# Another order of TensorE, VectorE and ScalarE between the down projection and the column a, and one z product moved ahead of the last output projection

## The reference

```
x = x + tanh(g_xattn[0]) * xattn0(layernorm(x), ctx)   # 32 heads of 128, 8 kv heads, rmsnorm on q and k, softmax
x = x + tanh(g_ffn[0])   * ffn0(layernorm(x))          # permute features, 16 blocks 32->128, gelu, 128->32, unpermute
x = x + tanh(g_xattn[1]) * xattn1(layernorm(x), ctx, ctx)
x = x + tanh(g_ffn[1])   * ffn1(layernorm(x))          # 8 experts 512x512, the best of 8 for each token

def xattn1(inp_q, inp_k, inp_v):                       # inp_k = inp_v = ctx, c = 128 channels (tokens), 8 groups of 16
    t, p, g = Wt @ inp_v, Wp @ inp_q, Wg @ inp_k       # for each batch, 128x128 times 128x512
    att = sum(p * g) over each group                   # one number for each batch and group
    y = blockdiag(Wz) @ (att * t)
    yn = (y - mean(y)) * rsqrt(var(y) + 1e-5)          # over each group
    return yn * gn_w + gn_b + inp_v
```

## Time and profile before

| | us |
|---|---|
| median of 3 runs | 797.38 (796.01, 797.38, 799.69) |
| profiled execution, its own time | 797.66 |
| its span (first to last instruction) | 795.9 |
| mean granted clock of TensorE | 0.982 |

### The profile page before, as it was taken

The page is one execution under the profiler, slowest core; times in us unless marked ns, Lnnn a source line. Parts: engine busy times, 40 slices in busy tenths (PEclk is TensorE's granted clock), DMA queues, the critical chain, the costliest instruction groups (busy, mean ns, idle before and its releaser), DMA issues.

```text
span 795.9 us, 12734 instructions
## 1 busy us (share of the span) xinstructions
PE 755.1 (95%) x3975; PEld 592.2 (74%) x3975; DVE 459.6 (58%) x1038; ACT 430.5 (54%) x1274; POOL 274.5 (34%) x431
## 2 busy tenths in 40 slices
PE   5999989899999999999999999999999987987997
PEld 3888877788888888888888888888887743555775
DVE  4786411556465656564655565656558764787652
ACT  4543315556556556555655655655555466557831
POOL 0331005234334233424423523433322438624242
PEclk9999999999999999999999999999999999797999
DMA  8545461132041140140131203203142135664232
GB/s 303 180 133 172 133 189 46 49 150 76 15 173 37 57 173 28 54 183 15 66 119 80 66 30 158 80 15 120 34 131 85 54 109 184 240 261 158 73 109 76
DMA packets 42126, 87.82 MB, mean 110 GB/s; under 512 B 5561, under 2 KB 26041, under 8 KB 38226
## 3 DMA queue, kind: packets, MB, share of 16 engines
q1 hardware_dynamic: 38884, 78.71, 28.7%
q0 software_dynamic: 3184, 8.41, 3.1%
HBM read 70.28 MB, written 35.57 MB: 133 GB/s over the span
## 4 chain that ended last, share of the span: by engine, by line
PE 71%; DVE 6%; ACT 3%; POOL 2%; DMA 2%; issue 1%; POOLq 0%; DVEq 0%; SPq 0%
PE banks L882 8%; PE banks L916 7%; PE banks L884 7%; PE banks L883 7%; PE banks L918 7%; PE banks L917 7%; PE banks L868 6%; PE banks L903 3%; PE banks L895 2%; PE banks L1831 2%; PE banks L1830 2%; PE banks L1832 2%; PE banks L927 2%; PE banks L929 2%; PE banks L928 2%
## 5 line engine op out<-in xcount | busy, mean ns | idle before, releaser
L592 ACT ACTIVATE p_sb<-p_sb,nmax 128x128 f32<-128x128 f32 x256 | 99.7, 391 | 62.7 <-DVE nmax L784 62.5
L587 ACT ACTIVATE oT_hi<-banks 128x512 fp32r<-128x512 f32 x64 | 38.2, 597 | 140.1 <-PE banks L929 140.1
L822 DVE SCALAR_TENSOR_TENSOR x_sb<-banks,tgates,x_sb 128x512 f32<-128x512 f32 x64 | 48.0, 749 | 70.8 <-PE banks L918 70.8
L690 POOL TENSOR_TENSOR v_lo<-v_raw,v_hi 128x128 fp32r<-128x128 f32 x64 | 29.5, 461 | 133.6 <-ACT v_hi L635 133.6
L779 DVE SCALAR_TENSOR_TENSOR p_sb<-banks,q_rstd,mask 128x128 f32<-128x128 f32 x256 | 71.5, 342 | 4.5 <-POOL q_rstd L83 4.0
L868 PEld LDWEIGHTS banks<-kT,qT_sb 128*128 128x128 f32 x512 | 67.7, 193 | 5.9 <-issue 0.5
L695 POOL TENSOR_TENSOR p_sb<-p_sb,rsum 128x512 f32<-128x512 f32 x64 | 66.5, 1040 | 15.2 <-DVE rsum L812 15.2
L868 PE MATMUL banks<-kT,qT_sb 128*128 128x128 f32 x512 | 68.2, 277 | 0.1
L768 DVE TENSOR_TENSOR oT_lo<-banks,oT_hi 128x512 fp32r<-128x512 f32 x64 | 44.1, 689 | 33.0 <-ACT oT_hi L587 33.0
L400 PE MATMUL banks<-w_hi,ctx_hi 128*128 128x512 f32 x128 | 54.1, 422 | 9.0 <-DVE ctx_lo L331 9.0
L816 DVE TENSOR_TENSOR pT_lo<-banks,pT_hi 128x512 fp32r<-128x512 f32 x64 | 44.2, 690 | 24.9 <-ACT pT_hi L610 24.9
(11 more groups left out here) (276 smaller groups left out, 1901.9 us busy)
## 6 DMA issues: line engine op xcount, KB each, us to landing
sorted_x<-in_empty SPq DMA_DIRECT2D x8, 2064.0 KB, 9.7
w_raw<-in_wq_l SPq DMA_DIRECT2D x8, 1024.0 KB, 5.1
w_raw<-in_wo_l SPq DMA_DIRECT2D x8, 1024.0 KB, 4.8
exp_w<-in_exp_w_l SPq DMA_DIRECT2D x8, 1024.0 KB, 9.3
kT_scr<-kT_st SPq DMA_DIRECT2D x16, 256.0 KB, 2.3
v_scr<-v_st SPq DMA_DIRECT2D x16, 256.0 KB, 2.3
xs<-sorted_x SPq DMA_DIRECT2D x15, 258.0 KB, 2.8
v_raw<-v_scr SPq DMA_DIRECT2D x14, 256.0 KB, 2.6
```

The costliest lines, as they stand in the source:

```text
L592: last = act.activation(p_sb[:, b % 2, h * P:(h + 1) * P], p_sb[:, b % 2, h * P:(h + 1) * P], ACT.Exp, bias=nmax[:, b % 2, h:h + 1], accum ...
```

## The change

The z product of batch 4 moves from the start of `middle` to a place ahead of the last output projection, into bank 6. On PE the gate weights and z means move ahead of y 0 to 3, and g 3 to 7 are put between the transposes of y. On DVE the gate column and the squares move ahead of the updates of x, and the first product moves behind all updates. On ACT the centring of z is put between the copies of g, and the third's seeds and the normalisations follow later in the list, two batches at a time. `normalise3` waits for the same things as before. Two waits of SP change places.

PE's order is now: g 0, 1; gate weights and z means; g 2; y 0 to 3; g 3; y 4, 5; g 4; y 6; g 5; y 7; p 0; g 6; p 1; g 7; p 2, 3; variance; p 4 to 7.

```diff
@@ attention
-        xT_ps, z_ps = [s.ps[i] for i in (0, 1, 4, 5)], [s.ps[i] for i in (0, 3, 0, 1)]
+        xT_ps, z_ps = [s.ps[i] for i in (0, 1, 4, 5)], [s.ps[i] for i in (0, 3, 0, 1, 6)]
...
+            def z4(u, b, g, odd):
+                if after(u, b, g, B - 1):
+                    pe.wait_ge(pT_lo_done, UNITS)
+                    z_product(4)
...
-                [(scores, 0), (sum_squares, 4), (z01, 0), (p_transpose, -1), (z2, -1), (o_proj, -2),
+                [(scores, 0), (sum_squares, 4), (z01, 0), (p_transpose, -1), (z2, -1), (z4, -2), (o_proj, -2),
                  (transpose_x, -4), (values, -1), (z3, -1)])
@@ middle, scalar
-            def normalise3(c):
-                act.wait_ge(xshift3_done, c + 1)
-                for b in range(*THIRDS[c]):
+            def normalise3(*bs):
+                for b in bs:
+                    act.wait_ge(xshift3_done, 1 if b < HB else b // 2)
                     reached(act, p_done, b - HB + 1)
...
-            for b in range(5):
-                copy_g(b)
+            copy_g(0)
+            copy_g(1)
+            copy_g(2)
+            centre(0, 1)
+            copy_g(3)
+            centre(2, 3, 4)
+            copy_g(4)
+            centre(5)
+            copy_g(5)
+            centre(6)
             seed3(0)
-            copy_g(5)
+            normalise3(0, 1)
+            seed3(1)
+            normalise3(2, 3)
             copy_g(6)
-            normalise3(0)
-            seed3(1)
-            centre(0, 1)
-            normalise3(1)
+            seed3(2)
+            normalise3(4, 5)
             copy_g(7)
-            seed3(2)
-            centre(2)
-            normalise3(2)
-            centre(3, 4, 5, 6, 7)
+            normalise3(6, 7)
+            centre(7)
@@ middle, vector
-            updates_with_stats(dve, s, update_x, x_done, bn_done, mv_done, xval3_done, THIRDS[:1])
-            negate_mean(0)
             dve.wait_ge(gmean_done, 1)
...
-            updates_with_stats(dve, s, update_x, x_done, bn_done, mv_done, xval3_done, THIRDS[1:2])
-            negate_mean(1)
-            product(0)
-            updates_with_stats(dve, s, update_x, x_done, bn_done, mv_done, xval3_done, THIRDS[2:3])
-            negate_mean(2)
-            for b in range(1, B):
+            for c in range(3):
+                updates_with_stats(dve, s, update_x, x_done, bn_done, mv_done, xval3_done, THIRDS[c:c + 1])
+                negate_mean(c)
+            for b in range(B):
@@ middle, tensor
-            pe.wait_ge(s.pT_lo_done, UNITS)
-            z_product(4)
             pe.wait_ge(s.oT_lo_done, UNITS)
             z_product(5)
...
             pe.wait_ge(yT_copied, PACKS)
-            for b in range(HB):
-                transpose_y(b)
             pe.wait_ge(zmv_done, B)
...
             pe.matmul(sm_ps[:, 0:B], s.group_mean[:, :], s.zmv[:, :, 0], start=True, stop=True).then_inc(gmean_done, 1)
-            for b in range(2, 6):
-                g_product(b)
+            g_product(2)
+            for b in range(HB):
+                transpose_y(b)
+            g_product(3)
             transpose_y(4)
             transpose_y(5)
+            g_product(4)
+            transpose_y(6)
+            g_product(5)
+            transpose_y(7)
+            p_product(0)
             g_product(6)
-            p_product(0)
-            transpose_y(6)
-            transpose_y(7)
+            p_product(1)
             g_product(7)
-            p_product(1)
             p_product(2)
@@ experts, sync
+            sp.wait_ge(bias_zeroed, 1)
             sp.wait_ge(s.recycled, 1)
-            sp.wait_ge(bias_zeroed, 1)
```

## The result

| | before | after |
|---|---|---|
| median, us (20 runs each, same chip) | 797.37 (792.41 to 799.69) | 799.35 (796.82 to 800.42) |
| profiled execution: own time, span | 797.66, 795.9 | 797.5, 795.7 |

What follows compares the result with a forecast made beforehand. The bound was taken as the loop over all engines from seed3(0) to the last product. Later p 0 (693.0), 9.1 us of products and 1.95 for low clock gave +3.4 us, forecast 801.0, range 799.0 to 803.5.

Steps and rivals of the forecast that it cites:

- The moved z product: PE ahead of the last output projection: fills a 0.81 us idle; value 0, idle before x transposes grows to 2.1.
- The front part: Gate weights, z means, g 2 ahead of y: PE idle 1.4 us, not 3.37; y 0 to 3 at full clock.
- the updates come 5 us sooner: DVE's updates of x: about 5 us sooner in readiness, update 4 at 682.4 instead of 687.43.
- The held seed: ACT's seed3(0) waits behind copy_g(5) and centre(6): logarithm at 690.2 instead of 686.62, p 0 at 693.0.
- The clock: PE behind y: clock falls before g 5, stays low 3.9 us from p 0, losing 1.95 us of work.
- From p 0 to the last product: PE does ten products without a gap: 9.1 us, plus 1.95 for the low clock.
- The sum: Last product at 704.05 instead of 700.66: +3.4 us on the profiled execution, 801.1; forecast 801.0.
- The first: ACT and POOL bound, clock back at p 0 or never fallen: +0.9 us, 798.3; chance 0.16.
- The third: Clock up, seed not held if y's third load lands before 685.1: 794.3 at 682.0; smaller form 796.5; chance 0.16.
- The fourth: A later stage hides the column a, so nothing changes: 797.4; chance 0.04.

Runs made afterwards that it cites:

- 6: After with seed3(0) alone moved straight behind copy_g(4) on ACT, PE's list untouched: 795.72 us, 1.0013 [0.9993, 1.0033] to before.
- 7: Before with seed3(0) alone put behind copy_g(5) and copy_g(6) on ACT: 796.59 us, 1.0031 [1.0009, 1.0052] to before.
- the third experiment: After with g 5 ahead of y 6 on PE and seed3(0) ahead of centre(5, 6) on ACT: 793.75 us, 0.9994 to before.
- 5: Before with gate weights, z means and g 2 ahead of y, and DVE's gate column and squares ahead of the updates: 795.32 us, 1.0009.
- the eleventh: Before with only g 2 moved ahead of y and 10 idle matmuls: 794.30 us, 0.9983 [0.9961, 1.0005] to before.
- after, run again: The changed kernel itself, measured and profiled again on another chip: 798.95 us, 1.0053 [1.0034, 1.0073] to before.
- 2: After with 8, 12 and 15 idle matmuls (results unread) behind g 3, g 4 and y 7: 800.57 us, 1.0083 to before.
- the eighth: After with g 5 and seed3(0) early, plus 7, 8, 9 idle matmuls ahead of y 0, behind g 3 and g 5: 800.49 us, 1.0088 to before.

## Why the prediction was right, and where it was not

- **The moved z product: right as far as seen.** No cost showed; an idle of 1.86 did nothing to the clock. I had computed that idle as 2.1.
- **The front part keeps the clock at y: right in most profiles, the idle not as computed.** I computed 1.4 us of idle ahead of y; it was 0 in after and 2.88 in the second profile of after, where the clock fell at 675.5. What was wrong is what I took to follow: that the updates come 5 us sooner. From the mark, third 0 is ready at +40.8 as before, because PE's updates of the semaphores behind y and g come late.
- **The held seed: right, and shown to be the main cost,** together with the low clock that its wait can bring. The seed waited for copy_g(5), that for g 5, that for y 6, that for the third load. Taking it away gave 3.2 us (6), adding it to before cost 2.4 (7). From y 6 (682.41) to the logarithm (685.07) it took 2.66; my step at full clock gives 0.5 + 0.87 + 0.25 + 0.50 + 0.63 = 2.75. The third load came earlier than I took it: issued at +38.8 from the mark, where before had +40.2. That is 1.4 us off the forecast.
- **The clock: right in kind, wrong in place.** I let it fall before g 5. It stayed up behind idles of 2.19 and 3.08 and fell only in the wait for p 0, so the 1.3 us (0.42 + 0.87) of slow y 6 and g 5 were not lost. The Trainium skill ("TensorE: Matmul & The Clock Gate", section "What's actually happening") has the low clock as the state of rest, which activity releases; the trace agrees in direction, but the length of an idle did not tell when: 3.08 left the clock alone here, and it fell within an idle of 1.85 in the third experiment (0.5 from about 676.2).
- **From p 0 to the last product:** 12.2 us (687.88 to 700.05) where I had 11.05; the clock was low for 6 us of it instead of 3.9.
- **The sum:** the term that was mis-sized is the time from the mark to p 0. I had 693.0 - 641.9 = 51.1; it was 48.3, 2.8 less: 1.4 from the earlier load and 1.3 from the clock that stayed up. With 1.1 more behind p 0, +3.4 became +1.7 at the last product and 2.1 at the end. Against the median of before, 797.37, that makes 799.5; measured were 799.35.
- **Where the loss lies, and the luck in the number.** I had 2.93 of the 3.4 us ahead of p 0 and 0.46 behind it. In the profile it is 0.15 ahead and 1.58 behind, so the hold of the seed did not delay p 0 against this execution of before, and two misses of opposite sign partly cancel. After's second profile is nearer to the forecast: p 0 at +50.7 (2.5 later than before's), the last product at +61.5 (2.8 later). The median of 799.35 lies 0.35 us above the lower end of my range, 799.0; after's second median, 798.95 on another chip, lies just below it. That the number fitted is in part luck.
- **The rivals.** The first (lists alone, +0.9) is refuted in its condition, since the products did run slow. The third (a load before 685.1 makes it faster) had its condition met and was wrong: from the mark the threshold is +43.2, and the load landed at some +42.7 (682.3 in after). After was slower all the same, because the seed stayed held and the clock fell in the wait for p 0. The fourth (it does nothing) is excluded by the interval, [1.0023, 1.0053].
- **What I did not see:** the kernel before has a faster form, without the fall at 675. On the chip of experiments 5 to 7, where before's median was 794.19, the change costs more, 1.0053 [1.0034, 1.0073] or some 4 us; against the faster form alone it would be more again. A profile with a low clock in the stretch under study should have been read as one of two cases.

**A kernel that beats both** is the fourth: the kernel before with 14 idle matmuls in the wait for y, 0.9978 [0.9964, 0.9991], 792.60 against 794.38 for before on that chip (after was not run there; it had 1.0038 and 1.0053 elsewhere). It is the best of eleven variants, so its gain may be flattered; the eleventh, with a like filling, had 0.9983 [0.9961, 1.0005].

## What to carry to other kernels

An in-order list couples what stands in it: before moving a small instruction that starts a long loop (here a logarithm) behind another, ask which load that other one waits for. Here the first step stood ready for 4.7 us behind such a hold, and TensorE, which then waited 3.5 us, lost its clock as well. And where a profile shows a low clock at the place of the change, look at the times and mean clocks of all runs before taking that execution as the baseline.

## What the runs showed of the hardware

- The clock fell at idles of 1.85 (3), 2.05 (7), 2.88 (after, run again), 3.34 (7), 3.37 (before) and 3.52 us (after), and did not at 1.86, 2.19 and 3.08 (all three in after) nor at 2.53 (6) and 2.85 (5). It then stayed low for 3.4 to 10.2 us; 6.8 in after, with PE full from 687.9.
- PE's semaphore updates can be recorded up to 4 us behind the ends that the profile models for its matmuls, several of them within 0.1 us (three at 681.51 to 681.59 in 5), and ACT and DVE, which wait for them, then go on within 0.04 us of each other; the profile says "remote" for some of these waits. What it is, and whether it goes with the front part, stayed open.
- Idle matmuls have effects of their own: ahead of y on before they gained 0.2%, in after's lists they gained nothing (2), and with them the eighth had 1.0088 where the third had 0.9994 without, on another chip. In the eighth's profile the first update starts 4 us late. Why is open.
